# Graph layer on one core: the third batch of cross one-hots moves from ScalarE to VectorE

## The reference

```
xn = layernorm(x)
x  = x + (segment_sum(weight * xn[src], dst) @ gnn_W.T + gnn_b) + mix(xn)
x  = x + moe(layernorm(x))        # 16 experts, two chosen for each node
```

## Time and profile before

| | |
|---|---|
| median of 3 runs | 1254.11 us (1252.87 to 1254.82) |
| profiled execution | 1253.87 us, its span 1252.1 us |
| TensorE matmuls busy | 1089.7 us, 87% of the span |
| VectorE busy | 801.4 us, 64% |
| ScalarE busy | 673.9 us, 54% |
| GpSimd busy | 612.3 us, 49% |
| mean granted TensorE clock | 0.942 of full speed |

### The profile page before, as it was taken

One profiled execution on the slowest core, in us unless ns is written; L12 is line 12 of the kernel. 1 busy time (PEld: TensorE's weight loads), 2 busy tenths in 40 slices (PEclk: granted clock), 3 DMA queues, 4 the chain that ended last, 5 costly groups with the idle time before them and its releaser, 6 DMA issues.

```text
span 1252.1 us, 21128 instructions
## 1 busy us (share of the span) xinstructions
PE 1089.7 (87%) x6319; PEld 946.1 (76%) x6319; DVE 801.4 (64%) x1896; ACT 673.9 (54%) x1623; POOL 612.3 (49%) x625
## 2 busy tenths in 40 slices
PE   6797899899998999989999998816999999999990
PEld 5575677677776787767777787716999999999980
DVE  7875678888888888888888877663222222222226
ACT  4467597898978979789797874311111111011000
POOL 5937556576665756757657570001333333333320
PEclk9899799999999999999999999557999999999995
DMA  7214222232222322223223230325999999999948
GB/s 220 87 30 126 63 75 78 76 92 76 87 84 73 92 74 85 86 72 92 77 81 89 75 102 6 103 75 187 328 333 333 334 331 334 330 330 335 338 167 307
DMA packets 113486, 196.08 MB, mean 157 GB/s; under 512 B 13505, under 2 KB 61439, under 8 KB 113407
## 3 DMA queue, kind: packets, MB, share of 16 engines
q1 hardware_dynamic: 84073, 120.62, 28.7%
q0 software_dynamic: 26112, 71.34, 18.1%
q10 hardware_dynamic: 3222, 3.20, 0.7%
HBM read 177.12 MB, written 17.99 MB: 156 GB/s over the span
## 4 chain that ended last, share of the span: by engine, by line
PE 49%; DVE 17%; ACT 10%; DVEq 8%; issue 7%; POOL 3%; DMA 3%; ACTq 2%; SPq 0%; POOLq 0%
PE psum L1027 18%; PE psum L1037 9%; PE psum L952 7%; ACT in_slot L412 4%; DVE agg L1288 4%; POOL arena L690 3%; PE psum L883 3%; DVE agg L1294 3%; PE psum L961 2%; PE psum L873 2%; ACT first_use L426 1%; DVE agg L1669 1%; PE psum L983 1%; DVEq L1135 1%; DMA arena<-y_rows,gather_i 1%
## 5 line engine op out<-in xcount | busy, mean ns | idle before, releaser
L690 POOL DMA_INDIRECT arena<-y_rows,gather_i x416 | 439.4, 1056 | 250.9 <-PE psum L952 71.6
L952 PE MATMUL psum<-arena,hot 128*128 128x256 f32 x832 | 217.3, 390 | 16.5 <-issue 6.7
L623 ACT ACTIVATE arena<-psum 128x512 f32<-128x512 f32 x64 | 38.2, 597 | 326.9 <-PE psum L1027 326.9
L1288 DVE TENSOR_TENSOR agg<-psum,agg 128x256 f32 x416 | 174.9, 420 | 55.4 <-DVE agg L1288 30.4
L952 PEld LDWEIGHTS psum<-arena,hot 128*128 128x128 f32 x832 | 150.0, 191 | 51.8 <-issue 30.0
L1027 PEld LDWEIGHTS psum<-arena 128*128 128x128 f32 x1536 | 181.2, 194 | 4.9 <-issue 2.5
L529 ACT ACTIVATE arena<-arena,listed 128x256 f32<-128x256 f32 x416 | 172.6, 495 | 21.5 <-DMA arena<-y_rows,gather_i 21.4
L1027 PE MATMUL psum<-arena 128*128 128x128 f32 x1536 | 181.7, 277 | 2.0 <-DVE arena L1626 2.0
L961 PE MATMUL psum<-arena,first_use 128*128 x624 | 159.5, 391 | 25.6 <-ACT first_use L428 25.2
L1633 DVE TENSOR_TENSOR arena<-psum,arena 128x512 f32<-128x512 f32 x64 | 44.3, 692 | 204.7 <-PE psum L1027 204.7
L706 POOL DMA_INDIRECT chosen_rows<-arena,back_at x64 | 63.2, 987 | 219.9 <-DVE arena L1640 215.1
(11 more groups left out here) (224 smaller groups left out, 1664.0 us busy)
## 6 DMA issues: line engine op xcount, KB each, us to landing
arena<-in_L_ffn_w_dram SPq DMA_DIRECT2D x144, 512.0 KB, 5.7
xnT<-in_L_ffn_w_dram SPq DMA_DIRECT2D x48, 512.0 KB
arena<-y_rows,gather_i POOLq DMA_INDIRECT x416, 2.8
arena<-chosen_rows SPq DMA_DIRECT2D x4, 1280.0 KB, 9.9
y_rows<-w ACTq DMA_DIRECT2D x6, 512.0 KB, 2.9
agg<-in_x_dram SPq DMA_DIRECT2D x4, 640.0 KB, 6.8
n_rows<-arena SPq DMA_DIRECT2D x4, 640.0 KB
out_dram<-agg SPq DMA_DIRECT2D x4, 640.0 KB
```

What stands on the lines that cost most here:

```text
L690: pool.indirect_dma_start(rows[h][:, t, :], None, y_rows, bass.IndirectOffsetOnAxis(ap=gather_i[h][:, t:t + 1], axis=0)).then_inc(gathered ...
L952: pe.matmul(bank_of(g, t // 2)[:, (t % 2) * C:(t % 2 + 1) * C], hot[:, (g * GT + t) % HOTS, :], rows[h][:, t, :], start=True, stop=True).t ...
L1288: dve.tensor_tensor(own, bank_of(g, t // 2)[:, (t % 2) * C:(t % 2 + 1) * C], own, ALU.add).then_inc(evicted, 1)
```

## The change

ScalarE makes only the batches 0 and 1 of a group's cross one-hots. Batch 2 is made by VectorE with one is_equal over eight matrices, `last_hots(g)`, after the eviction of step 41 and ahead of step 42's other work; TensorE waits for it with a semaphore of its own before step 48. The offsets of this batch are kept in `last_picked` with the other sign, one more small subtraction in `keep_picked`. `cross_hots` has room for three batches, so ScalarE's wait for the use of the first batch is gone.

```
-        first_use = sb("first_use", [P, 5 * COLS])
+        first_use = sb("first_use", [P, CROSS * P])
...
             def cross_hot(g, b):
-                k = g * (CROSS // BATCH) + b
                 act.wait_ge(picks_kept, g + 1)
-                if b == 2:
-                    act.wait_ge(met, g * STEPS + GT + BATCH)
-                elif g >= 1:
-                    act.wait_ge(met, (g - 1) * STEPS + GT + (b + 2) * BATCH)
-                its = slice(k % 2 * BATCH, (k % 2 + 1) * BATCH)
+                if g >= 1:
+                    act.wait_ge(met, (g - 1) * STEPS + GT + (b + 1) * BATCH)
+                its = slice(b * BATCH, (b + 1) * BATCH)
...
                 std(1, g)
-                cross_hot(g, 2)
                 if sorts:
                     slot_hot(g + 2, 3)
...
                     if b % BATCH == 0:
-                        pe.wait_ge(cross_hot_ready, (g * CROSS + b) // BATCH + 1)
+                        if b < 2 * BATCH:
+                            pe.wait_ge(cross_hot_ready, 2 * g + b // BATCH + 1)
+                        else:
+                            pe.wait_ge(last_hot_ready, g + 1)
...
             def keep_picked(g):
                 dve.wait_ge(list_picked, g + 1)
+                dve.tensor_tensor(last_picked[g % 2][:, :], picked_list[:, 2 * BATCH:CROSS], bin_base[:, 2 * BATCH:CROSS], ALU.subtract)
                 dve.tensor_tensor(picked[g % 2][:, :], bin_base[:, :], picked_list, ALU.subtract).then_inc(picks_kept, 1)
+
+            def last_hots(g):
+                dve.tensor_tensor(cross_hots[:, 2 * BATCH:CROSS, :], iota[:, :].unsqueeze(1).to_broadcast([P, BATCH, P]),
+                                  last_picked[g % 2][:, :].unsqueeze(2).to_broadcast([P, BATCH, P]), ALU.is_equal).then_inc(last_hot_ready, 1)
...
                         evict_pair(g, (step - GT) // 2)
+                    if step == 42:
+                        last_hots(g)
                     beside(g, step)
```

More of the change, by code:

```diff
@@ L122, in gps_layer @@
         relu_h = sb("relu_h", [P, HC, 2 * P])
-        first_use = sb("first_use", [P, 5 * COLS])
-        assert 2 * BATCH * P <= 5 * COLS
+        first_use = sb("first_use", [P, CROSS * P])
+        assert 5 * COLS <= CROSS * P
         edge_i = first_use[:, 0:2 * COLS].bitcast(I32).rearrange("p (a c) -> p a c", a=2)
@@ L128, in gps_layer @@
         weight_in = first_use[:, 4 * COLS:5 * COLS]
-        cross_hots = first_use[:, 0:2 * BATCH * P].rearrange("p (b c) -> p b c", c=P)
+        cross_hots = first_use[:, 0:CROSS * P].rearrange("p (b c) -> p b c", c=P)
         pieces = sb("pieces", [P, COLS // 2, FIELDS, 2], BF16)
@@ L163, in gps_layer @@
         picked = [sb(f"picked{h}", [P, CROSS]) for h in range(2)]
+        last_picked = [sb(f"last_picked{h}", [P, BATCH]) for h in range(2)]
+        assert CROSS == 3 * BATCH
         bin_of = [sb(f"bin_of{h}", [1, GT], I32) for h in range(2)]
@@ L248, in gps_layer @@
         scaled = sem("scaled")
-        cross_hot_ready, d_root = sem("cross_hot_ready"), sem("d_root")
+        cross_hot_ready, last_hot_ready, d_root = sem("cross_hot_ready"), sem("last_hot_ready"), sem("d_root")
         list_kept, list_turned, listT_kept, list_picked, picks_kept = (
@@ L417, in cross_hot @@
             def cross_hot(g, b):
-                k = g * (CROSS // BATCH) + b
                 act.wait_ge(picks_kept, g + 1)
-                if b == 2:
-                    act.wait_ge(met, g * STEPS + GT + BATCH)
-                elif g >= 1:
-                    act.wait_ge(met, (g - 1) * STEPS + GT + (b + 2) * BATCH)
-                its = slice(k % 2 * BATCH, (k % 2 + 1) * BATCH)
+                if g >= 1:
+                    act.wait_ge(met, (g - 1) * STEPS + GT + (b + 1) * BATCH)
+                its = slice(b * BATCH, (b + 1) * BATCH)
                 for j in range(BATCH):
-                    act.activation(cross_hots[:, k % 2 * BATCH + j, :], iota[:, :], ACT.Abs, bias=picked[g % 2][:, b * BATCH + j:b * BATCH + j + 1])
+                    act.activation(cross_hots[:, b * BATCH + j, :], iota[:, :], ACT.Abs, bias=picked[g % 2][:, b * BATCH + j:b * BATCH + j + 1])
                 act.drain()
@@ L957, in add_up @@
                     if b % BATCH == 0:
-                        pe.wait_ge(cross_hot_ready, (g * CROSS + b) // BATCH + 1)
+                        if b < 2 * BATCH:
+                            pe.wait_ge(cross_hot_ready, 2 * g + b // BATCH + 1)
+                        else:
+                            pe.wait_ge(last_hot_ready, g + 1)
                     if b % 2 == 0:
                         pe.wait_ge(evicted, evictions_before(g, unit))
-                    pe.matmul(bank_of(g, unit)[:, (b % 2) * C:(b % 2 + 1) * C], cross_hots[:, (g * CROSS + b) % (2 * BATCH), :],
+                    pe.matmul(bank_of(g, unit)[:, (b % 2) * C:(b % 2 + 1) * C], cross_hots[:, b, :],
                               rows[h][:, bass.ds(row_of[b], 1), :].rearrange("p t c -> p (t c)"),
```

## The result

The changed kernel takes 1265.64 us (median of its runs, 1263.8 to 1266.63) against 1253.8 us in the runs of the kernel before beside it: a ratio of 1.0103, 95% interval 1.0088 to 1.0117, so it is 1% slower. The profiled execution took 1266.63 us, 12.8 us above the one of before (1253.87); the forecast for it was 1266.9 us.

A forecast was written before the change was run, and what follows sets the result against it. VectorE, never waiting in groups 1 to 10, was taken as the bound: 10 x 1.23 = 12.3 us, plus 0.5 for group 11, gives 12.8 us on 1253.87, so 1266.9 us; range 1261 to 1274.

The forecast's parts named there:

- ScalarE's loss: Eight Abs and one Relu a group leave ScalarE, about 3.5 us; worth nothing to VectorE.
- Groups 11 and 12: Last two groups: group 11 costs 0.5 us (between 0 and 0.9), group 12 costs 0 (between -1.1 and +1.1).
- its two paths: To group 12's first std: VectorE's extra 1.23 us less its 0.90 wait leaves 0.3; or gathers stretched 0 to 0.9, taken 0.5.
- (1): TensorE's waits for ScalarE's L428 are gone; waits under 1 us for the new VectorE operation replace them.
- (2): VectorE's stretch from register load to register load is 52.7 us in groups 1 to 10, 45.4 us busy.
- (3): In groups 1 to 10 VectorE still has no wait for another engine over 0.3 us.
- (5): ScalarE's idle time grows.
- (4): TensorE's waits for the message at step 1 grow from under 1 to over 3 us.
- B: VectorE's 8.7 us of waits are truly TensorE's; an earlier TensorE gives 9.7 us back: 1257.2 us; chance 0.06.
- C: TensorE's pause moves to next group's step 1, grows to about 3.4 us and costs clock: 1278 us; chance 0.10.
- D: TensorE is the bound and VectorE has room; the step-48 waits go, 20.8 us: 1233.3 us; chance 0.05.
- E: VectorE's new work falls into unseen gaps, TensorE's gain goes in later waits: no difference, 1254 us; chance 0.05.

The follow-up runs named there:

- the first experiment: Kernel before with the third batch of cross one-hots made by no engine, steps 48 to 55 reading the first again: 1319.53 us, ratio 0.9987 (chip B).
- removed work: Kernel before with the hots of steps 16 to 23 made by nobody, a constant matrix read instead: 1250.46 us on chip A, 1331.92 us on chip C.
- the three exchanges: The change itself (1.0103); ScalarE making VectorE's hots of steps 16 to 23 in the kernel before (1.0008, chip B) and in the changed kernel (1.0057, chip C).

## Why the prediction was right

**The bound.** The step on which all rests, that VectorE has no gap in groups 1 to 10, held: an operation added to VectorE costs about its duration (0.97 to 1.10 us a group, alone on chip A), a second one costs the same again (on chip C), and 1.7 us added to TensorE cost nothing there. It was incomplete in one point. I had the 0.76 us between ScalarE's std and VectorE's reciprocal in group 9 and used it only to price ScalarE's loss at nothing. It also says that another chain is only that much shorter than VectorE's, and in other groups only 0.35 us. For a change that adds to VectorE that does not matter. For one that takes away from it, the same reading would have forecast 12 us and measured 3.

**The terms of the sum.** They can be read off as the start of the same VectorE instruction (a reciprocal, in one row a `hot_batch`) in both traces, after minus before:

| place | shift, us | forecast of the step |
|---|---|---|
| group 0, step 42 (before: 176.20) | -1.33 | 0 for the change |
| group 10, step 42 (694.10) | +11.02 | 12.3 more |
| group 11, step 42 (739.21) | +12.14 | |
| group 12, first std (755.34) | +11.50 | |
| group 12, hots at 763.04 | +11.13 | 0.5 for group 11 |
| group 12, step 42 (776.98) | +12.25 | |
| after the loop (788.44) | +12.28 | 0 for group 12 |
| end of the span | +12.7 | 0 |

Groups 1 to 10 took 12.35 us more, 1.235 each, against 1.23. The two instructions, in the changed kernel's timeline of VectorE:

```profile
650.60 1.22 DVE L1209 TENSOR_TENSOR first_use<-iota,last_picked 128x1024 f32<-128x1024 f32 x1
651.74 0.15 DVE L1356 RECIPROCAL stat<-stat 128x2 f32<-128x2 f32 x1
...
674.88 0.16 DVE L1205 TENSOR_TENSOR last_picked<-psum,bin_base 128x8 f32<-128x8 f32 x1
674.96 0.17 DVE L1206 TENSOR_TENSOR picked<-bin_base,psum 128x24 f32<-128x24 f32 x1
```

1.14 us from the start of `last_hots` to the next instruction (1.13 taken), 0.08 for the subtraction (0.10 taken). Group 0 is right too: the shift is -1.32 us before its step 42 (at the eviction that starts at 174.11 in the trace of before) and -1.33 after, so the wait of the earlier trace rows hid the operation. The -1.3 us itself has nothing to do with the change: it arises at about 125 us, where a group of TensorE's matmuls took 2.13 us in the trace of before and 1.17 in that of after. The granted clock of the stretch 125.48 to 130.00 is 0.68 before and 1.00 after; TensorE had stood for 2.9 to 3.0 us just ahead in both.

Groups 11 and 12 are the terms that were mis-sized: 0.5 and 0 forecast, 0.11 and 1.15 measured. In group 11 `last_hots` cost 1.12 us, and 0.64 came back at the std for which VectorE had waited 0.90 us, by the route that the prediction gave. Another 0.37 came back at 758.88 of before, where VectorE had one more wait for TensorE, of 0.57 instead of the usual 0.21 us, which I had not counted. The gathers were hardly stretched on the way: one that was under way when `last_hots` started at 750.21 took 0.94 us, and the next, which met its end, 1.14, not the 1.86 of the earlier trace rows.

```profile
751.11 1.14 POOL L688 DMA_INDIRECT arena<-y_rows,gather_i  x1 [0.30 <-PE psum L962]
```

In group 12 the operation costs all of its length:

```profile
788.09 1.22 DVE L1209 TENSOR_TENSOR first_use<-iota,last_picked 128x1024 f32<-128x1024 f32 x1
```

TensorE's wait of 1.09 us is gone there, but the last evictions stand behind the operation on VectorE and then run back to back, without the 0.17 to 0.24 us for which each waited for TensorE before. That brings 0.34 us back, and a gap of 0.44 us without a named releaser right after the loop takes it again. The bounds of the term were +-1.1, and the 0 between them was the wrong choice: with the change the end of the loop hangs on VectorE's last evictions, not on TensorE's last matmul. The range's lower bound for the last two groups, -1.6, was 0.3 too low by the prediction's own terms, since the later of its two paths was never under 0.3; the range that follows hardly changes. That the profiled execution came within 0.3 us of the forecast, 1266.63 against 1266.9, owes something to luck: -1.3 us at the start stands against +0.8 in the last two groups and +0.4 after the loop. The medians, over four executions each, differ by 11.8 us.

**The signs.** (1) held: waits for the new operation are 0.39 us each, 0.4 was said, as in TensorE's timeline here. (2) held nearly: 45.4 us busy as said, stretches of 52.94 to 53.33 us against 52.7, which was reckoned from the shortest group of before; from the mean of 51.76 it would have been 52.99, and 53.03 was measured. (3) held on the mean only: VectorE's waits for TensorE are 0.24 us each, but the longest is 0.6, as it is in the earlier trace rows, so the bound of 0.3 was set too tight; three more put down to L962, of up to 1.8 us, lie at the register load, which has cost 1.5 us with either name. (5) held: ScalarE is busy for 41.5 us of a stretch instead of 44.6. (4) was wrong in size:

```profile
651.96 1.12 PE L962 MATMUL psum<-arena,first_use 128*128 x4 [0.39 <-DVE first_use L1209]
655.38 1.13 PE L962 MATMUL psum<-arena,first_use 128*128 x4 [0.53 <-DVE agg L1300]
659.29 0.89 PE L950 MATMUL psum<-arena,hot 128*128 128x256 f32 x3 [0.57 <-DVE hot L1287]
661.84 0.66 PE L862 MATMUL psum<-ident,wv 128*128 128x128 f32 x4 [1.45 <-DVE wv L1335]
```

The time that TensorE is ahead is not handed over in one pause before the message (over 3 us said) but in five, the evictions' and the hots' first: 0.39, 0.53, 0.28 (at 656.79, not shown), 0.57 and 1.45.

**The rivals.** B (part of VectorE's waits is TensorE's) would have shown as a group below 52.7 us, and a TensorE made later by 1.7 us (extra matmuls) did not lengthen the group. C (the pause costs clock) lost its ground with sign (4), since no pause is longer than 1.8 us; the granted clock is 0.97 in some stretches after, as it was in some before, and the operation issued twice cost no more than linearly. D and E fall by the result, and D by the first experiment, which gives TensorE all it could want.

## What to carry to other kernels

Before work is moved from an engine with waits behind it to another, find out which engine never waits in the repeated stretch; busy shares (here 87% for TensorE, 64% for VectorE) pointed at the wrong one, because the waits of the busy one were all for the other. Then read the second number as well, the smallest lead, over several repetitions, of any value that this engine takes from the others (0.35 to 0.76 us here): adding to the bound costs nearly in full, but taking away from it pays at most that lead, and here it paid less (0.17 of 1.13 us a group). Here VectorE and the chain through GpSimd and ScalarE both stand within 1 us of a group's length, and none of the three exchanges between them that were measured came out below the kernel before.

## What the runs showed of the hardware

- The same kernel took 1253 us on one chip and 1322 and 1329 us on two others. VectorE's and ScalarE's busy time per group is nearly the same there; nearly all of the difference is one stall of some 5 us a group, for which the trace names no releaser, though the granted clock is a little lower too (0.925 on chip C against 0.94 for the changed kernel). Ratios held up for the change (1.0103 and 1.0109), less well for the added operation alone (1.0089 on chip A, 1.0065 on B), and not for removed work (0.9977 on A, 1.0018 on C).
- An eviction on VectorE that waits for the eviction ahead of it stands 0.21 us: 88 such waits, 18.6 us in nine groups of the changed kernel. They belong to VectorE's list of work as much as its busy time does, and no busy share shows them.
- TensorE's granted clock can differ between two executions at the same place of the same work: 0.68 against 1.00 over 4.5 us from 125.48, behind pauses of 2.96 and 2.92 us. It cost some 1.3 us there.
